# A transformer layer with routed experts on one core: softmax sums from a column of ones, and the query's feature map without its Relu pass

## The chip, the cores and the metric

The kernel runs on one core of a Trainium2 chip. The metric is device time in microseconds (us); lower is better. A core has TensorE (PE in the rows; its weight loads are PEld), VectorE (DVE), ScalarE (ACT), GpSimd (POOL) and SyncE (SP), which issues transfers. Each engine works through its own list in order, and the lists meet in semaphores.

## The reference

The input is 32 images of 36 patches. Each image becomes 37 tokens of 256 numbers (a class token ahead of the embedded patches). One attention layer follows, then a layer of experts; both add to their input. The attention part, for each head of 64 columns:

```python
aw = where(causal, q @ k.T, lowest)
attn = softmax(aw) @ v
sq = elu(q) + 1.0                          # exp(min(q, 0)) + max(q, 0)
A_mem = (sq @ mem) / (sq @ z + 1e-06)
out = sigmoid(betas) * A_mem + (1.0 - sigmoid(betas)) * attn
h = h + out @ Wo.T + bo
h = h + ffn(layernorm(h))                  # a shared expert, and the top 2 of 8
```

## The kernel before

**The tiles.** Three images are one tile of T = 111 tokens, so there are NT = 11 tiles, 0 to 10. The front of the kernel (about the first 140 us) embeds, normalises and attends, as a software pipeline written out by hand: in step s, `embed` works on tile s + 1, `project_qk` and `project_v` on tile s - 1, `scores`, `max_score`, `exps` and `finish_sq` on tile s - 2, `turn_prob`, `mix_values` and `combine` on tile s - 3, `turn_attn`, `project_out` and `residual` on tile s - 4, `turn_rows`, `row_lo` and `copy_x2_t` on tile s - 5, `logits` and `top2` on tile s - 6. Behind the last steps the order of the drain is written out call by call, mixed with the first work of the shared expert (`shared_up`, `shared_down`, `shared_lo`). Then come ten units of the shared expert, tables that sort tokens by expert, and 26 slot tiles of routed experts, whose rows are added to the output by indirect transfers.

**Attention of one tile.** PE writes the scores of the four heads into banks 0 and 7 (`scores`, L423 and L429). DVE takes the negated maxima (`max_score`, L1189). ACT runs `exps`: four Exp passes of 111x111 (L845), each with a bias per row and with `accum_out`, which gives the sum of the row; the compiled program has a second instruction, a read of the accumulator, behind each pass. PE transposes the exponentials (`turn_prob`, L438), ACT copies them back (L861), and PE multiplies by the values (`mix_values`, L517: four heads, two instructions each, 64 columns each) and then multiplies `sq` by the memory (L521). `mix_values(t)` waits for `prob_ready` of tile t + 1, since both use bank 7. DVE's `combine` adds 1e-6 to the memory's denominators (L1229), takes one reciprocal over them and the four row sums together (L1233, 8 numbers a row), multiplies by the gates (L1234), scales the memory's result and the attention's (L1235, L1242) and adds them (L1244).

**The query's feature map.** ACT's `tanh_q` makes three passes over 128x222 numbers, each waiting for the one before: Relu of -q (L894), Tanh (L898), and 1 - tanh (L902). DVE's `finish_sq` takes the reciprocal (L1209) and computes 2 x that + (max(q, 0) - 1) (L1213); the second term comes from POOL (`relu_q`, L1113).

**The order around them.** ACT's list in one step is `copy_prob_t`, a weight chunk's `split_hi`, `norm1`, `copy_qk`, `copy_v`, `copy_attn_t`, `norm2`, `exps`, `tanh_q`, `copy_x2_t`, `tanh_gap`, `copy_xln_t`; in steps 10 and 11 `copy_v` and `norm2` stand behind `exps`, and in step 10 `copy_xln_t` stands ahead of `copy_x2_t`. POOL computes the inverse standard deviations in six small dependent instructions (`inv_std`, L1099 to L1105). PE's list around the change in the drain is:

```python
            turn_xln(NT - 1)
            mix_values(NT - 4)
            turn_rows(NT - 6)
            turn_prob(NT - 3)
            logits(NT - 6)
            project_qk(NT - 1)
            turn_attn(NT - 4)
            scores(NT - 2)
            project_v(NT - 1)
            project_out(NT - 4)
            mix_values(NT - 3)
            turn_prob(NT - 2)
            shared_up(0, 0)
            turn_rows(NT - 5)
            turn_attn(NT - 3)
```

Of the kernel before, what the change touches and what calls it, by code (L numbers as in the profile page):

```python
# [57 lines left out]
def build(nc, patches, w_embed, embed_bias, w_qk, w_v, w_o, out_bias, betas, mem_z, w_ffn, w_gate,  # L58
# [3 lines left out]
    with ExitStack() as ctx:  # L62
# [3 lines left out]
        def sem(name):  # L66
            return ctx.enter_context(nc.semaphore(name))
# [59 lines left out]
        xln = part(2, D)  # L127
        xln_t = part(2, KC, T)
        qk_t = part(2, 4, T)
        v = part(3, D)  # L130
        q_min = part(2, 2, T)
        sq = part(3, 2, T)
        prob = part(2, HEADS * T)
        prob_t = part(2, HEADS * T)
# [78 lines left out]
        v_ready = sem("v_ready")  # L213
        qk_copied = sem("qk_copied")
        v_copied = sem("v_copied")
        q_min_ready = sem("q_min_ready")
        q_tanh_ready = sem("q_tanh_ready")
        q_den_ready = sem("q_den_ready")
        q_relu_ready = sem("q_relu_ready")
# [192 lines left out]
        def _(pe):  # L412
# [98 lines left out]
            def mix_values(t):  # L511
                pe.wait_ge(prob_t_ready, t + 1)
                pe.wait_ge(v_copied, t + 1)
                pe.wait_ge(sq_ready, t + 1)
                pe.wait_ge(prob_ready, min(t + 2, NT))
                for hd in range(HEADS):
                    nc.tensor.matmul(bank[7][0:T, hd * HD:(hd + 1) * HD],  # L517
                                     prob_t[0:T, t % 2, hd * T:(hd + 1) * T],
                                     v[0:T, t % 3, hd * HD:(hd + 1) * HD], start=True, stop=True)
                for k in range(KC):  # L520
                    mm = nc.tensor.matmul(bank[0][0:T, 2 * T + k * (P + 2):2 * T + (k + 1) * (P + 2)],  # L521
                                          sq[:, t % 3, k], s_mem_z[:, k], start=True, stop=True)
                mm.then_inc(mixed_ready, 1)
# [313 lines left out]
        def _(act):  # L837
            def exps(t):
                act.wait_ge(max_ready, t + 1)
                if t >= 2:  # L840
                    act.wait_ge(prob_turned, t - 1)
                for hd in range(HEADS):
                    src = bank[7 * (hd % 2)][0:T, (hd // 2) * T:(hd // 2 + 1) * T]
                    top_ = 2 * (hd % 2) + hd // 2
                    last = nc.scalar.activation(prob[0:T, t % 2, hd * T:(hd + 1) * T], src, ACT.Exp,  # L845
                                                bias=neg_max[0:T, t % 2, top_:top_ + 1],
                                                accum_out=mix[0:T, t % 4, HEADS + hd:HEADS + hd + 1])
                last.then_inc(prob_ready, 1)

            def copy_xln_t(t):  # L850
# [33 lines left out]
            def copy_v(t):  # L884
                act.wait_ge(v_ready, t + 1)
                if t >= 3:
                    act.wait_ge(mixed_ready, t - 2)
                nc.scalar.copy(v[0:T, t % 3], bank[6][0:T, 0:D]).then_inc(v_copied, 1)

            def tanh_q(t):  # L890
                act.wait_ge(qk_copied, t + 1)
                if t >= 2:
                    act.wait_ge(sq_ready, t - 1)
                nc.scalar.activation(q_min[:, t % 2].rearrange("p a b -> p (a b)"),  # L894
                                     qk_t[:, t % 2, 0:2].rearrange("p a b -> p (a b)"),
                                     ACT.Relu, scale=-1.0).then_inc(q_min_ready, 1)
                act.wait_ge(q_min_ready, t + 1)
                nc.scalar.activation(q_min[:, t % 2].rearrange("p a b -> p (a b)"),  # L898
                                     q_min[:, t % 2].rearrange("p a b -> p (a b)"),
                                     ACT.Tanh, scale=-0.5).then_inc(q_tanh_ready, 1)  # L900
                act.wait_ge(q_tanh_ready, t + 1)
                nc.scalar.activation(q_min[:, t % 2].rearrange("p a b -> p (a b)"),  # L902
                                     q_min[:, t % 2].rearrange("p a b -> p (a b)"),
                                     ACT.Copy, scale=-1.0, bias=1.0).then_inc(q_den_ready, 1)

            def split_hi(c):
                staged(act, c)
# [177 lines left out]
        def _(pool):  # L1085
# [30 lines left out]
            nc.gpsimd.memset(ones[:], 1.0).then_inc(ones_ready, 1)  # L1116
            link(nc.gpsimd.memset(half[:], -0.5))
            nc.gpsimd.memset(silu_warm[:], 0.0).then_inc(half_ready, 1)
            nc.gpsimd.memset(y[:, 2], 0.0).then_inc(dummy_zero, 1)
            for s in range(STEPS):  # L1120
                if s == 0:
# [55 lines left out]
        def _(dve):  # L1177
            steps_done = [0]

            def link(ins):  # L1180

                steps_done[0] += 1
                ins.then_inc(dve_step, 1)
                dve.wait_ge(dve_step, steps_done[0])
# [21 lines left out]
            def finish_sq(t):  # L1206

                dve.wait_ge(q_den_ready, t + 1)
                link(nc.vector.reciprocal(q_min[:, t % 2], q_min[:, t % 2]))  # L1209
                dve.wait_ge(q_relu_ready, t + 1)  # L1210
                if t >= 3:
                    dve.wait_ge(mixed_ready, t - 2)
                nc.vector.scalar_tensor_tensor(out=sq[:, t % 3], in0=q_min[:, t % 2], scalar=2.0,  # L1213
                                               in1=q_relu[:, t % 2], op0=ALU.mult,
                                               op1=ALU.add).then_inc(sq_ready, 1)

            def heads(ap):
                return ap.rearrange("p (a b) -> p a b", b=HD)
# [3 lines left out]

            def combine(t):

                dve.wait_ge(prob_ready, t + 1)
                dve.wait_ge(mixed_ready, t + 1)
                both = mix[0:T, t % 4]
                pairs = bank[0][0:T, 2 * T:2 * T + KC * (P + 2)].rearrange("p (k c) -> p k c", c=P + 2)
                nc.vector.tensor_scalar(both[:, 0:HEADS].rearrange("p (k c) -> p k c", c=2), pairs[:, :, P:],  # L1229
                                        1e-6, None,  # L1230
                                        ALU.add).then_inc(dens_ready, 1)
                dve.wait_ge(dens_ready, t + 1)
                link(nc.vector.reciprocal(both, both))  # L1233
                link(nc.vector.tensor_tensor(share[0:T], both, keep[0:T], ALU.mult))  # L1234
                nc.vector.tensor_tensor(  # L1235
                    read[0:T].rearrange("p (k a b) -> p k a b", k=KC, b=HD),
                    pairs[:, :, 0:P].rearrange("p k (a b) -> p k a b", b=HD),
                    share[0:T, 0:HEADS].rearrange("p (k a b) -> p k a b", k=KC, b=1).broadcast_to(
                        [T, KC, 2, HD]), ALU.mult)
                if t >= 2:  # L1240
                    dve.wait_ge(attn_turned, t - 1)
                link(nc.vector.tensor_tensor(heads(attn[0:T, t % 2]), heads(bank[7][0:T, 0:D]),  # L1242
                                             per_head(share[0:T, HEADS:]), ALU.mult))
                nc.vector.tensor_tensor(attn[0:T, t % 2], attn[0:T, t % 2], read[0:T],  # L1244
                                        ALU.add).then_inc(attn_ready, 1)
# [424 lines left out]
```

## Time and profile before

| what | value |
|---|---|
| median of 3 runs | 338.19 us (338.16 to 338.84) |
| the profiled execution | 338.38 us, of which the span from the first to the last instruction is 336.5 us |
| mean granted TensorE clock | 0.988 of full speed |
| PE busy | 317.9 us (94%) |
| DVE busy | 223.7 us (66%) |
| ACT busy | 187.4 us (56%) |
| POOL busy | 148.1 us (44%) |

The busy times are of the profiled execution. A duration in a timeline runs from the start of an instruction to its end, and neighbours on one engine overlap somewhat, so the distance from start to start is shorter than the duration. The note in brackets is the idle time of the engine before the instruction, and what ended it.

### The profile page before, as it was taken

The numbers are of one execution on the slowest core, as the hardware profiler recorded it, in microseconds if no ns is written. First come the engines' busy times: TensorE is split into PE (matmuls) and PEld (weight loads), VectorE is DVE, ScalarE is ACT, GpSimd is POOL, SyncE is SP. The second block draws the span as 40 slices with busy tenths as digits, with TensorE's granted clock in tenths as the row PEclk, the third lists the DMA queues.
The fourth block names the chain that finished last, engine by engine and source line by source line (L and its number), as shares of the span: only waits on it lengthen the run. The fifth ranks groups of instructions, "written<-read, shape, count | busy, mean of one in ns | idle before, by whom it ended". The sixth has DMA issues, their size and how long they took to land.

```text
span 336.5 us, 9653 instructions
## 1 busy us (share of the span) xinstructions
PE 317.9 (94%) x3378; PEld 269.0 (80%) x3378; DVE 223.7 (66%) x497; ACT 187.4 (56%) x407; POOL 148.1 (44%) x224
## 2 busy tenths in 40 slices
PE   7789999999998899899999999999999999999990
PEld 6677888888887789799998777777777877777870
DVE  0234887888978888699979768675555555555540
ACT  1137767788777897756587788762323233332320
POOL 0544535556655336501272163645535353534131
PEclk9899999999999999999999999999999999999997
DMA  7592333225233101591679878233232323242321
GB/s 251 160 313 81 105 106 105 82 85 199 90 90 83 37 28 32 135 313 25 132 210 290 248 229 223 37 62 63 37 62 35 62 35 63 35 62 35 33 29 20
DMA packets 18612, 36.36 MB, mean 108 GB/s; under 512 B 3301, under 2 KB 10952, under 8 KB 18568
## 3 DMA queue, kind: packets, MB, share of 16 engines
q1 hardware_dynamic: 12136, 27.71, 25.5%
q0 software_dynamic: 6432, 8.03, 15.8%
q8 instruction: 31, 0.51, 0.6%
q14 instruction: 13, 0.11, 0.1%
HBM read 28.52 MB, written 7.21 MB: 106 GB/s over the span
## 4 chain that ended last, share of the span: by engine, by line
PE 76%; DVE 9%; issue 4%; DMA 3%; POOL 3%; ACT 2%; POOLq 1%; SPq 0%; DVEq 0%; ACTq 0%
PE bank L766 20%; PE bank L779 14%; PE bank L472 9%; PE bank L497 7%; PE bank L781 6%; PE bank L564 3%; PE bank L507 3%; PE bank L605 2%; DMA out_rows<-y,add_id 2%; PE bank L517 2%; PE bank L429 2%; PE bank L553 2%; PE bank L530 2%; DVE hid_lo L1289 1%; PE bank L521 1%
## 5 line engine op out<-in xcount | busy, mean ns | idle before, releaser
L766 PEld LDWEIGHTS bank<-x_t,weights 128*128 x1248 | 87.4, 98 | 25.6
L766 PE MATMUL bank<-x_t,weights 128*128 128x128 f16 x1248 | 103.9, 219 | 0.0
L944 ACT ACTIVATE act_out<-bank 128x512 f32<-128x512 f32 (+2 forms) x72 | 42.0, 585 | 86.7 <-PE bank L766 72.9
L779 PE MATMUL bank<-weights,hid_hi 128*128 x192 | 73.3, 382 | 0.3
L1172 POOL DMA_INDIRECT out_rows<-y,add_id x26 | 42.5, 1636 | 70.1 <-DVE y L1477 52.8
L1289 DVE SCALAR_TENSOR_TENSOR hid_lo<-act_out,hid_hi 128x512 f16<-128x512 f32 (+2 forms) x72 | 48.7, 680 | 12.8 <-ACT hid_hi L955 11.4
L781 PE MATMUL bank<-weights,hid_lo 128*128 x192 | 52.3, 273 | 0.0
L1295 DVE SCALAR_TENSOR_TENSOR weights<-stage,weights 128x1024 f16<-128x1024 f32 x36 | 42.9, 1218 | 0.4 <-ACT weights L908 0.4
L908 ACT ACTIVATE weights<-stage 128x1024 f16<-128x1024 f32 x36 | 36.8, 1048 | 0.0
L472 PE MATMUL bank<-weights 128*111 128x256 f32 x132 | 32.6, 398 | 1.0 <-DMA weights<-in_w_embed 0.9
L1139 POOL DMA_INDIRECT slot_rows<-x_rows,gather_id x26 | 27.7, 1066 | 13.2 <-DMA out_rows<-y 5.4
L1099 POOL TENSOR_SCALAR weights<-weights 111x1 f32<-111x1 f32 x22 | 6.8, 311 | 53.8 <-DVE weights L1197 53.6
L1474 DVE TENSOR_SCALAR y<-bank,slot_gate 128x256 f32<-128x256 f32 x24 | 11.6, 482 | 26.6 <-PE bank L781 25.0
L472 PEld LDWEIGHTS bank<-weights 128*111 128x111 f32 x132 | 23.3, 183 | 7.4 <-DMA weights<-in_patches 1.6
L564 PE MATMUL bank<-x_t,weights 128*128 128x119 f16 (+1 forms) x480 | 27.8, 216 | 0.0
L605 PE MATMUL bank<-weights,hid_hi 128*119 128x256 f16 (+1 forms) x160 | 27.4, 273 | 0.2 <-DVE hid_lo L1289 0.2
L564 PEld LDWEIGHTS bank<-x_t,weights 128*128 128x128 f16 x480 | 26.2, 98 | 0.1
L1287 DVE TENSOR_SCALAR hid_hi<-act_out 128x512 f16<-128x512 f32 x35 | 14.8, 422 | 15.4 <-ACT act_out L944 15.4
L497 PE MATMUL bank<-weights 128*128 128x111 f32 x176 | 23.9, 292 | 1.0 <-ACT weights L854 0.9
L497 PEld LDWEIGHTS bank<-weights 128*128 128x128 f32 x176 | 21.9, 202 | 1.9 <-ACT weights L854 1.9
L955 ACT ACTIVATE hid_hi<-act_out 128x476 f16<-128x476 f32 (+2 forms) x37 | 22.8, 616 | 1.0
L1158 POOL DMA_DIRECT2D out_rows<-y x10 | 8.9, 889 | 31.8 <-DVE y L1491 27.1
(142 smaller groups left out, 549.7 us busy)
## 6 DMA issues: line engine op xcount, KB each, us to landing
stage<-in_w_ffn SPq DMA_DIRECT2D x36, 512.0 KB
weights<-in_patches SPq DMA_DIRECT2D x11, 333.0 KB, 3.1
x_rows<-rows SPq DMA_DIRECT2D x11, 111.0 KB
out_rows<-weights SPq DMA_DIRECT2D x10, 111.0 KB
out_rows<-y POOLq DMA_DIRECT2D x9, 119.0 KB, 5.8
weights<-in_w_embed SPq DMA_DIRECT2D x3, 256.0 KB, 3.6
weights<-in_w_qk SPq DMA_DIRECT2D x1, 512.0 KB, 5.5
slot_rows<-x_rows,gather_id POOLq DMA_INDIRECT x26, 3.7
```

Source lines behind the costliest of these rows:

```text
L472: mm = nc.tensor.matmul(embed_bank(t), s_patch[:, t % 2, k], s_we[:, k], start=(k == 0), stop=(k == PC - 1))
L497: mm = nc.tensor.matmul(bank[5][:, o * T:(o + 1) * T], s_wqk[:, k, o], xln_t[:, t % 2, k], start=(k == 0), stop=(k == KC - 1))
L564: mm = nc.tensor.matmul(o, weights[:, bass.ds(base + 2 * k * CHUNK + 2 * (col - col % D) + w * D + col % D, P)], x_of(2 * x + k), start=(k ...
L605: mm = nc.tensor.matmul(bank[down_bank(n)][0:m, 0:D], hid[:, n % 2, c * P:c * P + m], weights[:, at + w * D:at + (w + 1) * D], start=(c == ...
L766: mm = nc.tensor.matmul(o, weights[:, bass.ds(base + 2 * k * CHUNK + 2 * (col - col % D) + w * D + col % D, P)], x_t[:, b, (2 * x + k) * P ...
L779: nc.tensor.matmul(bank[5 + b][0:m, :], hid_hi[:, b, c * P:c * P + m], weights[:, bass.ds(at, 2 * D)], start=(c == 0), stop=False)
L781: mm = nc.tensor.matmul(bank[5 + b][0:m, 0:D], hid_lo[:, b, c * P:c * P + m], weights[:, bass.ds(at, D)], start=False, stop=(c == HC - 1))
L908: nc.scalar.mul(hi_of(c), staged_of(c), W_SCALE).then_inc(w_hi, 1)
L944: nc.scalar.activation(d_, s_, ACT.Silu, scale=1.0 / (X_SCALE * W_SCALE)).then_inc(hid_acted, 1)
L1172: nc.gpsimd.indirect_dma_start(out=out, out_offset=bass.IndirectOffsetOnAxis(ap=add_id[:, j:j + 1], axis=0), in_=y[:, y_place(j)], in_offs ...
L1289: nc.vector.scalar_tensor_tensor(out=four(hid_lo), in0=src, scalar=H_SCALE, in1=four(hid_hi), op0=ALU.mult, op1=ALU.subtract).then_inc(lo_ ...
L1295: nc.vector.scalar_tensor_tensor(out=lo_of(c), in0=staged_of(c), scalar=W_SCALE, in1=hi_of(c), op0=ALU.mult, op1=ALU.subtract).then_inc(w_ ...
```

## The change

The values `v` are stored with 65 columns for each head; the last is 1.0, written once at the start by POOL. `mix_values` multiplies by the 65 columns, so that bank 7 holds for each head 64 columns of the unscaled result and the row's sum. `exps` has no `accum_out` any more. `combine` takes the reciprocals of the sums from bank 7 in an instruction of its own, placed between the addition of 1e-6 and the reciprocal of the memory's denominators; it no longer waits for `prob_ready` itself. In `tanh_q` the Relu pass is left out: Tanh of q/2 is taken over all of q, then (1 - tanh)/2. `finish_sq` has the same two instructions, the second now with `min` in place of `mult`. The buffers that follow `v` lie 48 bytes further on in each partition.

```diff
-        v = part(3, D)
-        q_min = part(2, 2, T)
+        v = part(3, HEADS, HD + 1)
+        q_den = part(2, 2, T)
...
+                if t == 0:
+                    pe.wait_ge(v_ones, 1)
                 for hd in range(HEADS):
-                    nc.tensor.matmul(bank[7][0:T, hd * HD:(hd + 1) * HD],
+                    nc.tensor.matmul(bank[7][0:T, hd * (HD + 1):(hd + 1) * (HD + 1)],
                                      prob_t[0:T, t % 2, hd * T:(hd + 1) * T],
-                                     v[0:T, t % 3, hd * HD:(hd + 1) * HD], start=True, stop=True)
+                                     v[0:T, t % 3, hd], start=True, stop=True)
...
-                                                bias=neg_max[0:T, t % 2, top_:top_ + 1],
-                                                accum_out=mix[0:T, t % 4, HEADS + hd:HEADS + hd + 1])
+                                                bias=neg_max[0:T, t % 2, top_:top_ + 1])
...
-                nc.scalar.copy(v[0:T, t % 3], bank[6][0:T, 0:D]).then_inc(v_copied, 1)
+                nc.scalar.copy(v[0:T, t % 3, :, 0:HD],
+                               bank[6][0:T, 0:D].rearrange("p (a b) -> p a b", b=HD)).then_inc(v_copied, 1)
...
-                                     ACT.Relu, scale=-1.0).then_inc(q_min_ready, 1)
-                act.wait_ge(q_min_ready, t + 1)
-                nc.scalar.activation(q_min[:, t % 2].rearrange("p a b -> p (a b)"),
-                                     q_min[:, t % 2].rearrange("p a b -> p (a b)"),
-                                     ACT.Tanh, scale=-0.5).then_inc(q_tanh_ready, 1)
+                                     ACT.Tanh, scale=0.5).then_inc(q_tanh_ready, 1)
...
-                                     ACT.Copy, scale=-1.0, bias=1.0).then_inc(q_den_ready, 1)
+                                     ACT.Copy, scale=-0.5, bias=0.5).then_inc(q_den_ready, 1)
...
+            nc.gpsimd.memset(v[:, :, :, HD:], 1.0).then_inc(v_ones, 1)
...
-                nc.vector.scalar_tensor_tensor(out=sq[:, t % 3], in0=q_min[:, t % 2], scalar=2.0,
-                                               in1=q_relu[:, t % 2], op0=ALU.mult,
+                nc.vector.scalar_tensor_tensor(out=sq[:, t % 3], in0=q_den[:, t % 2], scalar=2.0,
+                                               in1=q_relu[:, t % 2], op0=ALU.min,
                                                op1=ALU.add).then_inc(sq_ready, 1)
...
-                dve.wait_ge(prob_ready, t + 1)
                 dve.wait_ge(mixed_ready, t + 1)
                 both = mix[0:T, t % 4]
+                mixed = bank[7][0:T, 0:HEADS * (HD + 1)].rearrange("p (a b) -> p a b", b=HD + 1)
...
+                nc.vector.reciprocal(both[:, HEADS:].rearrange("p (a b) -> p a b", b=1), mixed[:, :, HD:])
                 dve.wait_ge(dens_ready, t + 1)
-                link(nc.vector.reciprocal(both, both))
+                link(nc.vector.reciprocal(both[:, 0:HEADS], both[:, 0:HEADS]))
```

## Rows read from the trace of the kernel before

**Rows 1.** The page: the span, and each engine's busy time, share and instructions.

```profile
span 336.5 us, 9653 instructions
...
PE 317.9 (94%) x3378; PEld 269.0 (80%) x3378; DVE 223.7 (66%) x497; ACT 187.4 (56%) x407; POOL 148.1 (44%) x224
```

**Rows 2.** Windows: stretch, its length, busy us (instructions) of PE, PEld, DVE, ACT, POOL; PEclk, DMA, GB/s.

```profile
80.00:90.00 10.00, 10.00 (x78) 8.78 (x77) 8.80 (x24) 7.68 (x23) 5.77 (x15) 1.00 0.33 111
100.00:110.00 10.00, 9.06 (x70) 7.29 (x68) 8.67 (x23) 7.79 (x28) 5.93 (x10) 1.00 0.27 75
110.00:120.00 10.00, 8.63 (x105) 7.85 (x104) 8.92 (x26) 8.61 (x27) 3.19 (x7) 1.00 0.09 27
140.00:160.00 20.00, 20.00 (x279) 19.95 (x277) 18.05 (x58) 12.25 (x21) 3.13 (x4) 1.00 0.63 183
```

**Rows 3.** Chain that ended last, 50 to 65 us: start, duration, what.

```profile
54.52 0.96 PE bank L517 x8
...
64.45 0.74 PE bank L517 x8
```

**Rows 4.** Groups of instructions by line: count, busy us, mean ns, idle before.

```profile
L845 ACT ACTIVATION_READ_ACCUMULATOR weights<-bank,weights 111x1 f32 x44 | 8.9, 202 | 0.0
...
L517 PE MATMUL bank<-weights 111*111 111x64 f32 x88 | 10.1, 258 | 0.7 <-ACT weights L845 0.7
...
L1233 DVE RECIPROCAL weights<-weights 111x8 f32<-111x8 f32 x11 | 2.2, 204 | 0.4
```

**Rows 5.** Timeline of ACT, 100 to 105 us: start, duration, what, idle before.

```profile
100.37 0.35 ACT L845 ACTIVATE weights<-bank,weights 111x111 f32<-111x111 f32 x1 [0.91 <-DVE weights L1189]
100.62 0.19 ACT L845 ACTIVATION_READ_ACCUMULATOR weights<-bank,weights 111x1 f32 x1
100.72 0.34 ACT L845 ACTIVATE weights<-bank,weights 111x111 f32<-111x111 f32 x1
...
102.95 0.40 ACT L894 ACTIVATE weights<-weights 128x222 f32<-128x222 f32 x1
103.38 0.39 ACT L898 ACTIVATE weights<-weights 128x222 f32<-128x222 f32 x1
...
104.31 0.54 ACT L872 COPY x_t<-bank 128x444 f16<-128x444 f16 x1
```

**Rows 6.** Timeline of PE, 101 to 115 us.

```profile
101.96 0.96 PE L517 MATMUL bank<-weights 111*111 111x64 f32 x8 [0.26 <-ACT weights L845]
...
103.59 0.37 PE L485 MATMUL bank<-id,rows 111*128 111x111 f16 x4 [0.18 <-DVE rows L1260]
...
104.91 0.22 PE L543 MATMUL bank<-gate_pair,x_t 128*111 128x16 f16 x1 [0.50 <-ACT x_t L872]
...
110.47 0.96 PE L517 MATMUL bank<-weights 111*111 111x64 f32 x8 [0.45 <-ACT weights L845]
...
114.49 0.38 PE L449 MATMUL bank<-weights 111*128 111x111 f32 x2 [0.71 <-ACT x_t L872]
```

**Rows 7.** Timeline of DVE, 103 to 114 us.

```profile
103.14 0.39 DVE L1260 TENSOR_TENSOR rows<-weights,rows 111x256 f16<-111x256 f32 x1
...
113.46 0.43 DVE L1244 TENSOR_TENSOR weights<-weights 111x256 f32<-111x256 f32 x1
```

**Rows 8.** Chain that ended last, 124 to 129 us.

```profile
124.37 0.50 PE bank L521 x4
...
124.96 0.18 DVE weights L1229
...
125.16 0.21 DVE weights L1233
...
128.49 0.87 POOL weights L1099
```

**Rows 9.** Timeline of POOL: one line of code at two times.

```profile
99.39 0.27 POOL L1103 TENSOR_SCALAR weights<-weights 111x1 f32<-111x1 f32 x1
...
134.42 1.71 POOL L1103 TENSOR_SCALAR weights<-weights 111x1 f32<-111x1 f32 x1
```

More of the change, by code:

```diff
@@ L215, in build @@
         v_copied = sem("v_copied")
-        q_min_ready = sem("q_min_ready")
+        v_ones = sem("v_ones")
         q_tanh_ready = sem("q_tanh_ready")
@@ L893, in tanh_q @@
                     act.wait_ge(sq_ready, t - 1)
-                nc.scalar.activation(q_min[:, t % 2].rearrange("p a b -> p (a b)"),
+                nc.scalar.activation(q_den[:, t % 2].rearrange("p a b -> p (a b)"),
                                      qk_t[:, t % 2, 0:2].rearrange("p a b -> p (a b)"),
-                                     ACT.Relu, scale=-1.0).then_inc(q_min_ready, 1)
-                act.wait_ge(q_min_ready, t + 1)
-                nc.scalar.activation(q_min[:, t % 2].rearrange("p a b -> p (a b)"),
-                                     q_min[:, t % 2].rearrange("p a b -> p (a b)"),
-                                     ACT.Tanh, scale=-0.5).then_inc(q_tanh_ready, 1)
+                                     ACT.Tanh, scale=0.5).then_inc(q_tanh_ready, 1)
                 act.wait_ge(q_tanh_ready, t + 1)
-                nc.scalar.activation(q_min[:, t % 2].rearrange("p a b -> p (a b)"),
-                                     q_min[:, t % 2].rearrange("p a b -> p (a b)"),
-                                     ACT.Copy, scale=-1.0, bias=1.0).then_inc(q_den_ready, 1)
+                nc.scalar.activation(q_den[:, t % 2].rearrange("p a b -> p (a b)"),
+                                     q_den[:, t % 2].rearrange("p a b -> p (a b)"),
+                                     ACT.Copy, scale=-0.5, bias=0.5).then_inc(q_den_ready, 1)
             def split_hi(c):
@@ L1208, in finish_sq @@
                 dve.wait_ge(q_den_ready, t + 1)
-                link(nc.vector.reciprocal(q_min[:, t % 2], q_min[:, t % 2]))
+                link(nc.vector.reciprocal(q_den[:, t % 2], q_den[:, t % 2]))
                 dve.wait_ge(q_relu_ready, t + 1)
@@ L1241, in combine @@
                     dve.wait_ge(attn_turned, t - 1)
-                link(nc.vector.tensor_tensor(heads(attn[0:T, t % 2]), heads(bank[7][0:T, 0:D]),
+                link(nc.vector.tensor_tensor(heads(attn[0:T, t % 2]), mixed[:, :, 0:HD],
                                              per_head(share[0:T, HEADS:]), ALU.mult))
```

## The prediction

> **What bounds the kernel now.** I read the page first, then the windows, the chain that ended last, and at the places where that chain leaves PE the timelines of the engines. The page says that PE is busy 94% of a span of 336.5 us, DVE 66%, ACT 56% [rows 1]. The windows say where the rest lies. Between 80 and 90 us PE is busy for all 10.00 us while ACT has 7.68; there nothing that leaves ACT can be worth anything. Between 100 and 120 us PE is busy for 9.06 and 8.63 of each 10, and ACT and DVE have 7.8 to 8.9. From 140 us on PE is full again [rows 2]. So the change, which takes work off ACT in all 11 tiles, is paid only at those places of the front where PE waits for what ACT ends, and the question is which wait ends last at each of them. The granted clock is 1.00 in all four windows of [rows 2], so a few tenths of a microsecond less waiting should not change PE's rate.
>
> **What leaves ACT.** Two things. The 44 reads of the accumulator, 8.9 us busy in all [rows 4]; but what counts is the distance from start to start: an Exp begins at 100.37, its read at 100.62, the next Exp at 100.72 [rows 5]. The read costs 0.10 us, four of them 0.40 us a tile, for `prob_ready` and for all of ACT's list behind it. The Exp itself I leave at 0.25. Second, the Relu pass: 102.95 to 103.38, 0.43 us a tile [rows 5]. ACT's busy time should fall by 8.9 + 11 x 0.40 = 13.3 us, from 187.4 to about 174. I look for what it buys in order of time.
>
> **Tile 3's exponentials (54.5 us).** The chain counts 0.96 us for the eight instructions of `mix_values` at 54.52 and 0.74 for the same eight at 64.45 [rows 3]. `mix_values(2)` waits for `exps(3)`, which in this step alone stand behind a late `norm2(0)`. The other 0.22 us are that wait. With `prob_ready` 0.40 us earlier it is gone: gain 0.22, and no more, since PE then runs from its own list. All behind it is full PE, as between 80 and 90 us [rows 2], and moves along.
>
> **Step 10 (100 to 105 us).** Here ACT is in series: `exps(8)`, `copy_v`, `norm2(5)`, `tanh_q(9)`, `copy_xln_t(10)`, then `copy_x2_t(5)` at 104.31, for whose end PE waits before `logits(5)` at 104.91, 0.50 us idle [rows 5, 6]. ACT gets there 0.40 + 0.43 = 0.83 us sooner. But that is not passed on: `copy_x2_t(5)` needs `turn_rows(5)`, which PE starts at 103.59 because it waited for DVE's `row_lo(5)` (103.14 to 103.53) [rows 6, 7], and DVE comes to that through its own reductions and reciprocal, from which nothing is taken. `turn_rows(5)` ends at 103.59 + 0.37 = 103.96; the copy can start at about 104.0 in place of 104.31. Gain 0.3 of the 0.83. DVE's `row_lo(5)` is late next.
>
> **Step 11 (107 to 115 us).** `project_qk(10)`, `scores(9)` and `max_score(9)` follow in series on PE and DVE, all 0.3 sooner. Then PE waits 0.45 us for `exps(9)` before `mix_values(8)` at 110.47 [rows 6]. With the reads gone that starts another 0.40 sooner, 0.7 in all; PE's idle time just covers it. `shared_up(0, 0)`, `turn_rows(6)` and the copy that releases `turn_attn(8)` at 114.49 follow in PE's order, so 0.7 sooner, 113.79, if the other release of `turn_attn(8)` is there: `combine(8)` ends now at 113.46 + 0.43 = 113.89 [rows 7]. It is held by DVE's order and moves by 0.3 to 0.4 only, to about 113.55; with a semaphore's 0.1 to 0.15 us it arrives just in time. This is the tightest place of the sum.
>
> **The rest of the drain.** `scores(10)` goes 0.7 sooner, and DVE's chain behind it (`max_score(10)`, `finish_sq(10)`, `row_lo(7)`) with it; then PE's list up to `mix_values(10)`, whose last part is at 124.37, and `combine(10)` at 124.96 [rows 8]. `exps(10)` and the table load behind it are ahead of need. Here the change adds something on the chain: one reciprocal. Before, 8 numbers a row take 0.20 us [rows 4]; after, two times 4. The new one needs nothing but bank 7 and can run while DVE waits for the addition (124.96 to 125.16 [rows 8]). So it costs between nothing and a full 0.20; I take 0.05, near the lower end, as that wait is there in any case. From `residual(9)` POOL takes the chain at 128.49 [rows 8], then ACT and DVE, then PE is full again [rows 2]. Both PE's work and DVE's table work behind it begin from this chain, so the shift is kept, and the shift also moves the slot tiles and the last indirect transfers, which wait for y, not for a clock of their own.
>
> **Edits that I cost at nothing.** Other `combine`s: PE is full, or another wait ends later. The matmuls with 65 columns: eight instructions take 0.74 us [rows 3], 0.0925 each, with 64 columns and 111 stationary columns, while four instructions with 130 columns take 0.50 [rows 8], 0.125 each. If columns alone set the pace, 64 would take about 0.06 (half of 0.125), so the weight load sets it and a 65th column is covered; without the cover it is under 0.001 x 88 = 0.1 us. `copy_v` into runs of 64, `min` for `mult`, the dropped wait for `prob_ready` (implied by `mixed_ready`), and the ones written by POOL at the start, when it waits for statistics anyway: nothing, and at most 0.1 us if they were seen.
>
> **The sum.** 0.22 + 0.30 + 0.40 - 0.05 = 0.87 us. The profiled execution took 338.38 us (span 336.5), so 337.51 by its own time. It stood 0.19 above the median of the runs shown, 338.19, from which the same 0.87 gives 337.3. That is my forecast. No change and a change under 0.2% (0.68 us) are about what cannot be told apart here, so the sum lies just over that line.
>
> **Bounds of the Exp.** Below, the Exp might be no shorter in series without its read (gain 0 from it): then only the Relu pass counts, and it still fills the 0.3 that DVE leaves: 0.3, less 0.20 for a fully exposed reciprocal, is 0.1. Above, the Exp's own 0.25 might also shrink: PE's idle 0.45 at 110.47 plus the overlap of neighbours limits that place to 0.6, so 0.22 + 0.3 + 0.6 = 1.1 us.
>
> A rule weighed against these rows. The row shows 0.25 us from an Exp's start to its read and 0.35 to the next Exp [rows 5]. The Trainium skill, page "ScalarE: Activation LUTs", section "What ACT_TABLE_LOAD costs", gives an ACTIVATE as 186 ns + 0.833 ns an element, plus 93 ns for a pointer operand, with an overlap of 93 ns between neighbours. For 111 elements and one pointer that is an estimate of 0.28 us from start to start, so a read would save only 0.07, 0.28 a tile, and the sum by the page would be 0.75 us in place of 0.87. The sum goes by the row.
>
> **The rivals.**
> First, the read of the accumulator is not what holds `prob_ready`, or a second releaser stands right behind it (`turn_attn(8)` by `combine(8)`, where I found under 0.1 us of room). Then each place gives half or less, and the gain is 0.1 to 0.65; middle 337.8. For it: two of my three terms are already cut by DVE. Against: PE's two waits of 0.26 and 0.45 us name `exps` directly [rows 6].
> Second, POOL. In the drain its six small instructions lie on the chain, and one line takes 0.27 us at 99.39 and 1.71 at 134.42 [rows 9]; the difference must be something that it shares. If the 0.87 us shift changes how these meet DVE's work, one such stretch of 1.44 us comes or goes: 336.0 or 338.7. Against: POOL is started there by DVE itself (128.49 follows the statistics of `combine(10)`'s sequel), so both shift together.
> Third, slower: the 65-column matmuls are not covered by the weight load and run at the pace of the 130-column ones, 0.125 in place of 0.0925. All 88 [rows 4] lie on PE's full list or on the chain: 88 x 0.0325 = 2.9 us, less 0.87, gives 340.2. It decides from 0.87 / 88 = 0.010 us an instruction to the wrong side, and is measurably slower from 0.018. Only an odd width or a start off the former places speaks for it.
>
> **Chances.** The forecast 0.52 (its own range 337.1 to 337.6); the first rival 0.25; POOL 0.16, half to each side; the slower one 0.07. Faster by over 0.2%: the forecast, nearly all of it (0.50), and POOL's good half (0.08): 0.58. Within: the first rival and most of POOL's bad half: 0.32. Slower: 0.10. The range that leaves out the far halves and the slow case is 336.7 to 338.3.
>
> **What would show it.** ACT busy near 174 us with no reads of the accumulator and Exps still 0.25 apart or less; `mix_values(2)` at 0.74 in the chain; PE's wait before `logits(5)` at about 0.2 us in place of 0.50 and again named ACT, with `turn_rows(5)` still behind DVE; the wait of 0.45 before `mix_values(8)` near nothing; `combine(10)` no longer than 0.05 us more from its first to its third instruction; L517 with a mean near 258 ns. The prediction is wrong if L517 grows, if `turn_attn(8)` waits for L1244 in place of the copy, or if the POOL lines between 128 and 137 us have other lengths than now.

## The result, and the profile after

The changed kernel is faster by 0.37%: its median over 22 runs is 337.39 us against 338.59 us for 22 runs of the kernel before, and the ratio is 0.9963 with a 95% interval of 0.9947 to 0.9979. On 338.59 us that is 1.25 us, with an interval of 0.7 to 1.8 us. The forecast was 0.87 us.

In the rows of the kernel after some lines of code have moved: `mix_values` is L519 and L523 (L517 and L521 before), `exps` L847 (L845), `copy_x2_t` L873 (L872), `logits` L545 (L543), and POOL's third and fourth small instruction L1100 and L1101 (L1102 and L1103).

The page of the kernel after, the span and the busy times:

```profile
span 334.9 us, 9599 instructions
...
PE 316.8 (95%) x3378; PEld 268.3 (80%) x3378; DVE 224.1 (67%) x508; ACT 179.1 (53%) x352; POOL 150.4 (45%) x225
```

ACT's busy time fell by 8.3 us, not by the 13.3 of the prediction. Two groups of the kernel after by line say why (count, busy us, mean ns of one, idle before):

```profile
L847 ACT ACTIVATE weights<-bank,weights 111x111 f32<-111x111 f32 x44 | 11.9, 353 | 4.6 <-DVE weights L1188 4.5
...
L519 PE MATMUL bank<-weights 111*111 111x65 f32 x88 | 10.1, 257 | 0.1
```

The Exp (L847) has kept its mean, 353 ns. The reads were 8.9 us busy [rows 4], but each began before its Exp's record had ended (100.62 against 100.37 + 0.35 [rows 5]), so most of their time was already counted. The distance from start to start, by which the sum was made, is not touched by that. L519, the multiplication with 65 columns, has a mean of 257 ns against 258 [rows 4].

The window between 80 and 90 us, beside that of [rows 2]: stretch, length, and busy us of PE, PEld, DVE, ACT, POOL:

```profile
80.00:90.00 10.00, 10.00 (x80) 8.78 (x77) 8.80 (x26) 7.28 (x19) 6.24 (x15) 1.00 0.33 112
```

ACT has become emptier there, and PE is as full as before by this view. The chain that ended last, though, says more. The two places of [rows 3], in the kernel after:

```profile
54.01 0.74 PE bank L519 x8
...
63.66 0.74 PE bank L519 x8
```

The wait of 0.22 us at tile 3's exponentials is gone. But the second of these instructions now stands at 63.66 where it stood at 64.45, and 9.65 us behind the first in place of 9.93: 0.22 of that is the wait, the rest is something else. To find it, stretches of the two traces have to be compared between fixed marks.

**A ruler.** The spans of this kernel vary by more than a microsecond from run to run, most of it in the first 22 us (last section). So I use a ruler, a stretch between two marks that every trace has: on PE, from the first matmul of `turn_xln(1)` to the first matmul of `inverse()`: 143.10 us before (21.58 to 164.68) and 141.85 after (21.09 to 162.94). The difference, 1.25 us, is that of the timed runs; that it agrees to the hundredth is chance, since their interval is 1.1 us wide. What comes behind the ruler is 171.84 and 171.95 us in the two spans, 0.1 us more after, and 171.84 to 172.20 in all 13 profiles, so no gain or loss can be told there. The ruler in pieces, each between the starts of two PE calls:

| from, to | before | after | difference | in the prediction |
|---|---|---|---|---|
| `turn_xln(1)` to `turn_rows(0)` | 34.23 | 33.99 | -0.24 | -0.22 |
| to `project_qk(9)` | 40.80 | 40.39 | -0.41 | 0 |
| to `project_qk(10)` | 8.53 | 8.21 | -0.32 | -0.30 |
| to `mix_values(8)` | 5.33 | 4.97 | -0.36 | -0.40 |
| to `mix_values(10)` | 12.99 | 13.17 | +0.18 | 0 |
| to `inverse()` | 41.22 | 41.12 | -0.10 | +0.05 |
| sum | 143.10 | 141.85 | -1.25 | -0.87 |

**Steps 10 and 11, where the sum was made.** ACT's timeline after, which answers to [rows 5]:

```profile
99.23 1.09 ACT L847 ACTIVATE weights<-bank,weights 111x111 f32<-111x111 f32 x4 [0.91 <-DVE weights L1188]
100.19 0.39 ACT L889 COPY weights<-bank 111x256 f32<-111x256 f32 x1
...
101.44 0.41 ACT L896 ACTIVATE weights<-weights 128x222 f32<-128x222 f32 x1
101.88 0.39 ACT L900 ACTIVATE weights<-weights 128x222 f32<-128x222 f32 x1
...
102.86 0.54 ACT L873 COPY x_t<-bank 128x444 f16<-128x444 f16 x1 [0.36 <-PE bank L485]
```

Four Exps now go from 99.23 to 100.19, 0.24 us each in place of 0.33, and Tanh follows the row copies with no Relu between. PE's timeline after, which answers to [rows 6]:

```profile
102.45 0.37 PE L485 MATMUL bank<-id,rows 111*128 111x111 f16 x4 [0.54 <-DVE rows L1260]
...
103.45 0.22 PE L545 MATMUL bank<-gate_pair,x_t 128*111 128x16 f16 x1 [0.19 <-ACT x_t L873]
...
108.65 0.96 PE L519 MATMUL bank<-weights 111*111 111x65 f32 x8
...
112.68 0.38 PE L449 MATMUL bank<-weights 111*128 111x111 f32 x2 [0.71 <-ACT x_t L873]
```

PE's wait before `logits(5)` fell from 0.50 to 0.19 us, while the wait of `turn_rows(5)` for DVE's `row_lo(5)` rose from 0.18 to 0.54: DVE took over, as forecast. The wait of 0.45 before `mix_values(8)` has gone (108.65, no note), and `turn_attn(8)` still waits 0.71 for the copy of tile 6's rows, not for `combine(8)`.

**The piece that the prediction missed: steps 6 to 9.** From one `project_qk` to the next these four steps took 9.71 to 9.73 us each, and take 9.61 to 9.65. First DVE before, around `combine` and `top2` of one step, then PE before:

```profile
85.25 0.17 DVE L1229 TENSOR_SCALAR weights<-bank 111x4 f32<-111x4 f32 x1 [0.19 <-PE bank L521]
...
85.69 0.17 DVE L1234 TENSOR_TENSOR weights<-weights 111x8 f32<-111x8 f32 x1
...
88.52 0.16 DVE L1272 FIND_INDEX8 top_at<-top,logit 111x8 uint32<-111x8 f32 x1
```

```profile
84.49 0.65 PE L521 MATMUL bank<-weights 128*111 128x130 f32 x4
...
88.83 1.09 PE L507 MATMUL bank<-weights 128*111 128x256 f32 x4
```

Then the same of the kernel after, DVE and PE:

```profile
84.16 0.17 DVE L1228 TENSOR_SCALAR weights<-bank 111x4 f32<-111x4 f32 x1
84.23 0.17 DVE L1231 RECIPROCAL weights<-bank 111x4 f32<-111x4 f32 x1
84.35 0.18 DVE L1233 RECIPROCAL weights<-weights 111x4 f32<-111x4 f32 x1
84.57 0.17 DVE L1234 TENSOR_TENSOR weights<-weights 111x8 f32<-111x8 f32 x1
...
87.38 0.16 DVE L1272 FIND_INDEX8 top_at<-top,logit 111x8 uint32<-111x8 f32 x1
```

```profile
83.47 0.65 PE L523 MATMUL bank<-weights 128*111 128x130 f32 x4
...
87.73 1.05 PE L507 MATMUL bank<-weights 128*111 128x256 f32 x4
```

`project_v(8)` (88.83 before) began 0.15 us behind the end of `top2`'s index search (88.52 + 0.16), and in the kernel after at 87.73, 0.19 behind 87.54, hardly held any more. In steps 6 to 9 it waits for `top_done`, since it shares bank 6 with the logits. So DVE was the last to arrive at every step of a stretch in which PE's busy share was 10.00 of 10. The chain shows the wait as a longer `project_v`: of the kernel before in step 5, where it does not wait for `top_done`, and in step 9, then of the kernel after in step 9:

```profile
49.90 0.87 PE bank L507 x4
...
88.92 1.00 PE bank L507 x4
```

```profile
87.89 0.89 PE bank L507 x4
```

The wait was about 0.12 us, and a PE instruction's record of 0.2 us and more covers such a hole. Why DVE came sooner is seen at `combine`. The memory's last product ended at 84.49 + 0.65 = 85.14 before and `combine` began at 85.25, 0.11 us later; after, 83.47 + 0.65 = 84.12 and 84.16, 0.04 us. And from the addition to the gates' product it is 85.25 to 85.69, 0.44 us, before, and 84.16 to 84.57, 0.41 us, after.

The chain at `combine(10)`, which answers to [rows 8], shows the same in the drain:

```profile
122.73 0.50 PE bank L523 x4
...
123.25 0.17 DVE weights L1228
123.42 0.09 DVE weights L1231
123.51 0.14 DVE weights L1233
...
123.67 0.18 DVE weights L1234
```

The new reciprocal (L1231) adds 0.09 us to the chain and the old one (L1233) shrinks from 0.21 to 0.14, while the wait that stood between them is filled: 0.42 us in all in place of 0.44.

**The piece that came back: between `mix_values(8)` and `mix_values(10)`.** POOL's timeline after, two of the six small instructions for tile 7's norm, and DVE's at the same time:

```profile
111.44 0.35 POOL L1100 TENSOR_SCALAR weights<-weights 111x1 f32<-111x1 f32 x1
111.90 1.64 POOL L1101 TENSOR_SCALAR weights<-weights 111x1 f32<-111x1 f32 x1
```

```profile
111.90 0.46 DVE L1244 TENSOR_TENSOR weights<-weights 111x256 f32<-111x256 f32 x1
112.28 1.21 DVE L1295 SCALAR_TENSOR_TENSOR weights<-stage,weights 128x1024 f16<-128x1024 f32 x1
```

The fourth of the six takes 1.64 us. It begins as DVE starts an addition of two SBUF tensors and ends as DVE's weight split ends (112.28 + 1.21 = 113.49). In the kernel before, POOL met the split too, but one instruction later. Its fourth and fifth for tile 7:

```profile
113.34 0.27 POOL L1103 TENSOR_SCALAR weights<-weights 111x1 f32<-111x1 f32 x1
113.70 1.42 POOL L1104 TENSOR_SCALAR weights<-weights 111x1 f32<-111x1 f32 x1
```

There the fourth began 0.12 us ahead of the addition (113.46 [rows 7]) and got through, and the fifth waited for the split. Counted from the ruler's start, POOL's six instructions began 0.97 us sooner than before and DVE's addition 1.07 us sooner, since `combine(8)` had become shorter. So now the fourth is caught, two instructions stand behind the split's end in place of one, and the six take 3.75 us in place of 3.53. So `norm2(7)` on ACT, and with it the Exps of tile 10, the table load and all behind them came later against PE than before, until PE waited for ACT's copy of tile 7's rows ahead of `logits(7)`. The chain after:

```profile
119.65 0.43 ACT x_t L873
...
120.12 0.22 PE bank L545
```

Before, the chain ran through PE there without ACT.

### The profile page after: what moved, and what is told of

The parts are those of the page before. It is cut to its first block, busy times and chain, and to the rows that moved or that the text cites. A ratio compares the mean times of both kernels' runs of the same rounds, so it can differ in the third digit from the quotient of the medians.

```text
span 334.9 us, 9599 instructions
## 1 busy us (share of the span) xinstructions
PE 316.8 (95%) x3378; PEld 268.3 (80%) x3378; DVE 224.1 (67%) x508; ACT 179.1 (53%) x352; POOL 150.4 (45%) x225
## 4 chain that ended last, share of the span: by engine, by line
PE 75%; DVE 10%; POOL 4%; issue 4%; DMA 3%; ACT 2%; POOLq 1%; SPq 0%; DVEq 0%
PE bank L768 20%; PE bank L781 14%; PE bank L472 9%; PE bank L497 6%; PE bank L783 6%; PE bank L507 2%; PE bank L607 2%; DMA out_rows<-y,add_id 2%; PE bank L566 2%; PE bank L519 2%; PE bank L555 2%; PE bank L429 2%; PE bank L532 2%; DVE hid_lo L1289 1%; POOL weights L1101 1%
## 5 line engine op out<-in xcount | busy, mean ns | idle before, releaser
L472 PE MATMUL bank<-weights 128*111 128x256 f32 x132 | 33.5, 409 | 0.8 <-DMA weights<-in_w_embed 0.8
L472 PEld LDWEIGHTS bank<-weights 128*111 128x111 f32 x132 | 24.2, 189 | 7.3 <-DMA weights<-in_patches 0.9
L497 PE MATMUL bank<-weights 128*128 128x111 f32 x176 | 22.4, 280 | 1.0 <-ACT weights L855 0.9
L781 PEld LDWEIGHTS bank<-weights,hid_hi 128*128 128x128 f16 x192 | 18.5, 96 | 4.5 <-issue 1.4
```

The costliest lines, as they stand in the source:

```text
L472: mm = nc.tensor.matmul(embed_bank(t), s_patch[:, t % 2, k], s_we[:, k], start=(k == 0), stop=(k == PC - 1))
L497: mm = nc.tensor.matmul(bank[5][:, o * T:(o + 1) * T], s_wqk[:, k, o], xln_t[:, t % 2, k], start=(k == 0), stop=(k == KC - 1))
L781: nc.tensor.matmul(bank[5 + b][0:m, :], hid_hi[:, b, c * P:c * P + m], weights[:, bass.ds(at, 2 * D)], start=(c == 0), stop=False)
```

## The experiments

All rulers beside each other; the kernel that an edit starts from is named. Ratios are to the kernel before.

| run | from | ruler, us | median, us | ratio (95% interval) |
|---|---|---|---|---|
| e1, no own wait for `prob_ready` | before | 142.68 | 338.35 | 1.0001 (0.9979 to 1.0024) |
| e2, no Relu pass | before | 142.83 | 338.43 | 0.9984 (0.9964 to 1.0004) |
| e3, column of ones only | after | 142.07 | 338.17 | 0.9980 (0.9961 to 0.9998) |
| e4, wait put back | after | 142.03 | 337.98 | 0.9972 (0.9951 to 0.9993) |
| e5, before again | before | 143.11 | 339.91 (one) | |
| e6, `row_lo(5)` first | after | 141.71 | 337.47 | 0.9964 (0.9948 to 0.9981) |
| e7, 80 columns | after | 141.82 | 337.94 (one) | |
| e8, split of step 11 later | after | 141.64 | 337.36 | 0.9961 (0.9945 to 0.9978) |
| e9, e6 and e8 | after | 141.45 | 336.85 | 0.9948 (0.9922 to 0.9975) |
| e10, e9 and `top2(5)` first | after | 141.40 | 337.26 | 0.9954 (0.9934 to 0.9974) |
| e11, after again | after | 141.88 | 337.82 | 0.9977 (0.9956 to 0.9998) |

e5 and e11 say how well the ruler repeats: 143.10 and 143.11, 141.85 and 141.88. So 0.1 us can be read from one profile of the same program, where the intervals of whole runs are about 0.4% wide, 1.4 us. e11's own ratio of 0.9977, against 0.9963 for the same kernel in the first comparison, shows this too.

One piece of 0.17 us at the end of the ruler has nothing to do with what an edit is about. From `shared_down(0, 1)` on, all runs take the same time to `inverse()`, 37.23 to 37.25 us, but for e1, e3 and e4: 37.06 to 37.07. `inverse()` waits for tables that DVE makes, and the difference is idle time of DVE ahead of one comparison in `find_members`. Here the kernel after, then e4, which has no idle time noted:

```profile
139.92 0.54 DVE L1346 TENSOR_TENSOR weights<-s_iota,top_f 111x88 f32<-111x88 f32 x2 [0.20 <-DVE top_f L1344]
```

```profile
138.90 0.54 DVE L1347 TENSOR_TENSOR weights<-s_iota,top_f 111x88 f32<-111x88 f32 x2
```

In e1, e3 and e4 DVE's list up to there is 11 entries shorter or longer than in the ten other profiles, whose lists are all equally long: a wait more or less in each of 11 `combine`s, while the change takes out a wait and puts in an instruction. Why that moves the idle time is not shown. Up to `shared_down(0, 1)` the gains on the kernel before are 0.26 us (e1), 0.86 (e3), 0.91 (e4) and 1.24 (after).

**e1: only the dropped wait.**

```diff
-                dve.wait_ge(prob_ready, t + 1)
                 dve.wait_ge(mixed_ready, t + 1)
```

> The kernel before with one edit: combine does not wait for prob_ready itself (mixed_ready implies it). Ruler for all runs: from the first matmul of turn_xln(1) to the first of inverse() on PE, 143.10 us before and 141.85 after, which leaves out the uneven start. Theory: this wait is a step of its own in VectorE's list and costs 0.07 us a combine; combine stands ahead of top2, for which project_v waits in steps 6 to 9 (four matmuls 0.98 to 1.00 us in the chain, 0.88 to 0.92 after), so 0.06 + 3 x 0.07 there and 0.07 at combine(10): 0.3 us, ruler 142.8. Rival: the wait costs nothing and ScalarE's shorter list made those steps shorter: ruler 143.1.

The ruler fell by 0.42 us: 0.37 up to `project_qk(9)` (75.03 to 74.66 from the ruler's start) and 0.05 behind it. The four steps became 9.64 to 9.66 us, which is 0.07 to 0.08 less each; another 0.07 came ahead of them, at tile 3's exponentials. The 0.05 is a sum of larger pieces: 0.08 won at `combine(10)` and the 0.17 of `find_members`, less 0.19 lost between `mix_values(8)` and `mix_values(10)`. So the dropped wait alone is enough for the give-back that the kernel after has: POOL's fourth instruction begins 0.04 us ahead of DVE's addition (113.27 and 113.31) and takes 1.65 us. In e2, where `combine` is as before, it takes 0.27, and nothing is lost. The rival is out: ScalarE's list is that of the kernel before. That the median did not move (1.0001) says only that whole runs cannot show 0.4 us.

**e2: only the feature map.** The diff is that of the change in `tanh_q` and `finish_sq`.

> The kernel before with the new feature map alone: no Relu pass, Tanh over all of q, min in place of mult; accum_out, one reciprocal and combine's wait stay. Theory: it is worth 0.3 us in step 10, where ScalarE comes to copy_x2_t(5) 0.43 sooner but row_lo(5) cuts that, and nothing anywhere else: ruler 142.8, steps 6 to 9 as long as before (9.73 us). Rival: it is the Relu pass that lengthened steps 6 to 9: those steps 9.61 us, ruler 142.4 or less.

The ruler fell by 0.27 us, all of it between `project_qk(9)` and `project_qk(10)` (8.53 to 8.20 us, 0.06 of it given back later); the steps 6 to 9 stayed at 9.71 to 9.74. As expected.

**e3: the column of ones and the Exps without reads.** The kernel after with `tanh_q` and `finish_sq` of before, and with the wait.

> The kernel after, but with the three old passes of the feature map and with combine's wait for prob_ready: so the column of ones and the Exps without their reads alone. Theory: 0.22 at tile 3's exponentials, 0.3 in step 10 (0.40 from the reads, cut by row_lo(5)), 0.35 in step 11, and the two small reciprocals 0.03 shorter than the one in each place where combine counts (0.12): about 1.0 us, less up to 0.2 where GpSimd's inverse standard deviation of tile 7 is held by VectorE: ruler 142.1 to 142.3. Rival: without the Relu edit nothing of this is passed on at step 10, and the rest is lost to GpSimd: ruler 142.6.

Ruler 142.07, 1.03 us shorter than before, of which 0.17 is the idle time in `find_members`; the expectation did not have that piece. This one edit brings at steps 10 and 11 all that the three bring (0.32 and 0.36 us).

**e4: the kernel after with the wait.**

```diff
+                dve.wait_ge(prob_ready, t + 1)
                 dve.wait_ge(mixed_ready, t + 1)
```

> The kernel after with combine's wait for prob_ready put back. Theory: VectorE's start of combine is again about 0.1 us behind mixed_ready in place of 0.04, steps 6 to 9 get 0.06 longer each, combine(10) starts 0.07 later: ruler 141.85 + 0.3 = 142.15. Rival (the wait costs nothing): 141.85.

Ruler 142.03, 0.18 us longer than after; I had expected 0.3. But up to `shared_down(0, 1)` it is 0.33 us longer, as expected: 0.26 up to `project_qk(9)` and 0.07 at `combine(10)`. What makes the ruler's 0.18 of it is the idle time in `find_members`, which e4 lacks. The chain at `combine(10)` in this run shows the wait itself, a piece of DVE's queue that the chain after does not have:

```profile
121.81 0.50 PE bank L523 x4
...
122.34 0.02 DVEq L1225
...
122.41 0.16 DVE weights L1229
```

From the end of the matmuls to `combine` it is 122.31 to 122.41, 0.10 us, against 0.02 to 0.03 after. So the wait costs about 0.07 us wherever `combine` counts, in both kernels: in steps 6 to 9 it is 9.73 us with wait and single reciprocal, 9.65 without the wait (e1), 9.69 with wait and pair (e4), and 9.62 with neither cost (after). It is worth 0.33 us in the kernel after, and 0.26 in the kernel before, where leaving it out costs 0.19 at POOL. e3 and e4 differ by the feature map alone: 142.07 and 142.03. Beside the missing reads the Relu pass is worth 0.04 us, alone 0.27.

**e7: 80 columns a head.** `v` and bank 7 with 80 columns a head, 16 of them ones; one column of sums is read.

> The kernel after with 80 columns a head in place of 65 (16 of ones). Theory: a matmul of mix_values is paced by its weight load, 0.0925 us each, so 80 columns cost nothing: the eight instructions 0.74 us in the chain, ruler 141.85 within 0.1. Rival (columns count, by 0.84 us per 1000 columns and instruction as between wider ones): 15 x 0.00084 x 88 = 1.1 us more, ruler 142.9 and the eight at 0.84.

The group of these matmuls (count, busy us, mean ns):

```profile
L520 PE MATMUL bank<-weights 111*111 111x80 f32 x88 | 10.2, 259 | 0.1
```

15 columns more cost 2 ns in the mean of the record, the eight instructions take 0.75 us in the chain in place of 0.74, and the ruler stands at 141.82. So the number of columns does not set the pace of these matmuls up to 80, and the column of ones is free, which rules out the slower rival. That the weight load sets it is argued and not shown.

**e8: one weight split moved out of step 11.**

```diff
-        STEP_CHUNKS = [0, 0, 0, 1, 1, 1, 1, 1, 1, 1, 1, 1]
+        STEP_CHUNKS = [0, 0, 0, 1, 1, 1, 1, 1, 1, 1, 1, 0]
...
-        DRAIN_CHUNKS = 4
+        DRAIN_CHUNKS = 5
...
             hidden_hi(2, 1)
+            drain_hi(3)
             norm2(NT - 1)
...
             shared_lo(2, 1)
+            drain_lo(3)
             row_lo(NT - 1)
```

The former fourth drain split becomes the fifth, in its old place, and SP's loop loads one chunk more at its end.

> The kernel after, with the weight chunk of step 11 split later, in the drain (one split_hi and split_lo fewer in step 11, one more each between the second half of the shared expert's unit 2 and tile 10's last rows). Theory: in step 11 GpSimd's fourth small instruction for tile 7 takes 1.64 us because VectorE's split runs, so norm2(7), the Exps of tile 10 and ScalarE's list come 0.58 us late against the rest, which gave back 0.18 at logits(7). Without the split that instruction takes about 0.3 to 0.7, logits(7) is no longer held by ScalarE: ruler 141.85 - 0.18 = 141.67, if the place to which the split goes has room. Rival: GpSimd's 1.64 us has another cause and stays; or the later split costs up to 1 us at row_lo(10): ruler 141.85 to 142.8.

POOL in this run, the same two instructions:

```profile
111.71 0.34 POOL L1101 TENSOR_SCALAR weights<-weights 111x1 f32<-111x1 f32 x1
112.16 0.50 POOL L1102 TENSOR_SCALAR weights<-weights 111x1 f32<-111x1 f32 x1
```

0.50 us in place of 1.64, and the ruler is 141.64, 0.21 shorter (0.18 expected). From `mix_values(8)` to `mix_values(10)` it is 12.92 us, less than the 12.99 before, where POOL's fifth instruction still waited for the split. So DVE's work beside it had held POOL's instruction, and that was what gave back 0.18 us.

**e6, e9, e10: can more be had?** e6:

```diff
-                    residual(s - 4)
-                    row_lo(s - 5)
+                    if s == NT - 1:
+                        row_lo(s - 5)
+                        residual(s - 4)
+                    else:
+                        residual(s - 4)
+                        row_lo(s - 5)
```

> The kernel after, with VectorE's row_lo(5) ahead of residual(6) in step 10. Theory: in step 10 PE's turn_rows(5) waits 0.54 us for row_lo(5), which is late by VectorE's order and not by ScalarE's norm2(5), done 0.5 us earlier; so row_lo(5) comes about 0.45 sooner and copy_x2_t(5), logits(5) and all behind them too: ruler 141.85 - 0.4 = 141.45. Rival: residual(6) moves back by 0.9 us and with it GpSimd's statistics of tile 6, norm2(6) and step 11, which eats it: 141.8 or more.

A miss: 0.14 in place of 0.4. PE's timeline in e6:

```profile
100.95 0.37 PE L485 MATMUL bank<-id,rows 111*128 111x111 f16 x4 [0.16 <-DVE rows L1260]
...
105.47 1.09 PE L507 MATMUL bank<-weights 128*111 128x256 f32 x4 [0.32 <-DVE top_at L1272]
```

`turn_rows(5)` waits 0.16 in place of 0.54 and the way from `project_qk(9)` to `project_qk(10)` is 7.83 us in place of 8.21, 0.38 shorter, as expected, but then `project_v(10)` waits 0.32 for `top2(5)`: DVE's list did not become shorter, and PE only meets it later. The rival's way (tile 6's statistics and step 11) was not it either: from `mix_values(8)` to `mix_values(10)` it is 13.15 us, and 13.17 after.

> The kernel after with both edits: row_lo(5) ahead of residual(6), and the weight chunk of step 11 split later. The first alone shortened the ruler (first matmul of turn_xln(1) to first of inverse()) by 0.14 us, the second by 0.21. Theory: they act at different places (step 10, and logits(7)), so they add: 141.85 - 0.35 = 141.50. Rival: the first was cut by VectorE (project_v(10) waited 0.32 for top2(5)) and the second moves nothing of that, or they share the same slack: 141.6 to 141.65.

Ruler 141.45, 0.40 shorter where 0.35 was expected: the two add.

e10 puts `top2(5)` ahead of the weight split in DVE's step 10.

> As the last, and top2(5) stands ahead of the weight chunk's split_lo in step 10. Theory: project_v(10) no longer waits 0.32 us for top2(5), and VectorE comes to max_score(9) up to 0.15 sooner, so more of the 0.32 that row_lo first brought in step 10 is passed on: ruler 141.3 to 141.4. Rival: max_score(9), which sets exps(9) and mix_values(8), then waits for the split in place of top2, and nothing changes: 141.5.

Ruler 141.40. By the number this is at the edge of the theory's range, but it is only 0.05 us under e9, which two profiles cannot tell from nothing. PE no longer waits for `top2`, but `max_score(9)` now stands behind the split (it starts at 106.54, as the split that began at 105.41 ends) and sets the Exps, for which `mix_values(8)` waits 0.19 us. So the rival's mechanism is what the trace shows; from `project_qk(10)` to `mix_values(8)` 0.09 us was won against it.

> The kernel after, unchanged, on the same chip as the last two. All theories: ruler 141.85 within 0.05; its median beside theirs says whether 0.35 to 0.5 us on the ruler can be seen in whole runs (the start alone varies by 1 us or more, so I expect intervals that overlap).

Of the versions run, e9 and e10 have the shortest rulers, 1.65 to 1.7 us under before and 0.4 to 0.45 under after. In whole runs of one chip their ratios, 0.9948 and 0.9954, stand beside 0.9977 for the kernel after; the intervals overlap, so that part rests on the ruler.

## Why the prediction was right

Where and how the change pays was right, and two of its edits were costed wrong. The nearness of the number is in part luck. The forecast was 337.3 us and the median 337.39, because two misses cancel: the kernel before has a median of 338.59 us over 22 runs, 0.40 above the three that the forecast started from, and the gain in the medians, 1.20, is 0.33 above the 0.87. On the ruler it is 1.25 us, more than the 1.1 that the prediction gave as its bound above.

**What leaves ACT** was right by the distance from start to start: 0.24 us an Exp in place of 0.33, and 0.43 for the pass. As busy time it was wrong, 8.3 in place of 13.3 us, because records overlap. The figures of the Trainium skill, page "ScalarE: Activation LUTs", section "What ACT_TABLE_LOAD costs", had put an Exp at an estimated 0.28 us from start to start. The trace after has 0.24, so the row was the better guide here.

**Tile 3's exponentials**: 0.24 in place of 0.22. **Step 10**: 0.32 in place of 0.30, cut by `row_lo(5)` as written. Its 0.30 was put down to reads and Relu pass together, and e2 and e3 with e4 show that either alone brings it. **Step 11**: 0.36 in place of 0.40.

**"The rest of the drain"** had one term too much and missed one. The reciprocal that was to cost 0.05 costs nothing: the pair is 0.02 to 0.03 us shorter than the one, and the dropped wait saves 0.07 more. From `mix_values(10)` to `shared_down(0, 1)` it is 3.99 us before, 3.96 with the pair (e4), 3.91 without the wait (e1) and 3.89 after. And the sentence "`exps(10)` and the table load behind it are ahead of need" failed: POOL's fourth instruction for tile 7 was caught by DVE's work, as the second rival had it in general, though at 112 us and not between 128 and 137 us, where its lines are as long as before (1.71 us in both); it gave back 0.18 (e8). Against this rival the prediction had said that POOL and DVE shift together. They did not: 0.97 and 1.07 us, and 0.1 us was enough, since the kernel before had missed the addition by 0.12.

**"Edits that I cost at nothing"** holds the largest error. "Other `combine`s: PE is full", and the "nothing" for the dropped wait for `prob_ready`, are both wrong for the same reason: in steps 6 to 9 PE waited about 0.12 us a step for DVE, unseen in a busy share of 10.00. The dropped wait was a step of its own in DVE's queue, 0.07 us. The two together are the missing 0.41 us; e1 shows the wait's part (0.30 of it), e4 (9.69 us a step with the wait, against 9.73) that of the reciprocals. The 65th column did cost nothing (e7).

With -0.41 added, the give-back of 0.18 and -0.15 for the last piece (from +0.05 to -0.10), the forecast of 0.87 becomes 1.25 (the other terms differ by 0.00 in sum).

## What to carry to other kernels

A PE busy share of 100% does not prove that PE waits for nobody: compare one call's length in the steps where it must wait for something with its length in the steps where it need not (`project_v` took 0.87 us in the chain up to step 5 and 0.98 to 1.00 in steps 6 to 9). A semaphore wait that another wait implies is not free when it stands on an engine that is the last to arrive; here it cost 0.07 us each time. And where runs scatter by more than the change is worth, measure between two fixed instructions inside the trace, and look at the pieces between them: the sum of e4 was 0.15 us off what its edit did, by an idle time far behind it.

## What the runs showed of the hardware

**The start.** Most of the scatter of whole runs lies ahead of the ruler: of the 1.54 us between the spans of the kernel before and of e5, the same kernel, 1.17 lie there and 0.36 behind the ruler. Over the 13 profiles `turn_xln(1)` began between 19.90 and 22.78 us. Part of that is `project_qk(0)`, which began between 13.8 and 15.3 us. The rest is the stretch from there to `turn_xln(1)`: in seven profiles it took 7.7 us, in six 6.06, with the same instructions. Windows from 12 to 16 and 16 to 20 us of the kernel after, then e7 (PE's granted clock is the first number behind POOL's):

```profile
12.00:16.00 4.00, 1.86 (x13) 1.24 (x12) 1.04 (x3) 0.95 (x2) 2.64 (x8) 1.00 0.58 156
16.00:20.00 4.00, 4.00 (x25) 3.44 (x24) 0.00 (x0) 1.97 (x5) 2.71 (x6) 1.00 0.65 170
```

```profile
12.00:16.00 4.00, 1.86 (x14) 1.63 (x14) 1.03 (x3) 0.94 (x2) 2.64 (x9) 0.96 0.53 143
16.00:20.00 4.00, 4.00 (x16) 3.37 (x16) 0.00 (x0) 1.95 (x5) 2.34 (x5) 0.62 0.70 177
```

In the slower kind the granted clock averages 0.57 to 0.80 between 16 and 20 us, so part of it ran at 1.2 in place of 2.4 GHz; in the faster kind it is 1.00. Before it fell PE had been idle for parts of 12 to 16 us, but PE was as idle in the kernel after (1.86 us busy of 4.00), where it did not fall. Of the profiles of the kernel after and what derives from it, six are of the faster kind and three of the slower; the four of the kernel before and what derives from it are all of the slower. Yet the kernel before does not always start so: 9 of its 87 timed runs beside the experiments have spans of 334.8 to 335.6 us, which with the ruler's 143.10 and 171.84 behind it leave at most 20.7 us for the start, where the slower kind never took less than 21.58. What decides it stays open. It is worth 1.64 us, more than the change, and lies outside the ruler.

**POOL beside DVE.** One small instruction on 111 numbers takes 0.27 us alone, 1.64 us when DVE's addition and the weight split behind it, each of two SBUF tensors, run beside it, and 0.50 when only the short addition is there (e8). It ends as DVE's work ends each time, and does not get in between the two. The Trainium skill, page "SBUF — State Buffer", section "Who interferes with whom", has the rule that a VectorE instruction with two SBUF inputs contends with a GpSimd instruction that reads SBUF; by that rule, the trace agrees.
